# A ninth table looked up by products, gapless sample groups, and the move of the interactions cut into 36 two-dimensional parts

## What is computed

```python
e = jnp.stack([tbl_0[ids[:, 0]], ..., tbl_25[ids[:, 25]]], axis=1)   # 2048 x 26 x 128
combined = concatenate([e, r_dense_x[:, None, :]], axis=1)            # 2048 x 27 x 128
z = einsum('bfd,bgd->bfg', combined, combined)[:, TRIU_I, TRIU_J]     # 351 pairs, k=1
h = concatenate([z, r_dense_x], axis=1)                               # 479 columns
h = maximum(h @ W_top1 + b_top1, 0)                                   # 512
h = maximum(h @ W_top2 + b_top2, 0)                                   # 256
y = h @ W_top3
```

## Time and profile before

| | |
|---|---|
| median of 3 runs | 408.6 us (408.58 to 408.74) |
| the profiled execution | 406.5 us, span 404.7 us, mean granted clock 0.996 |
| TensorE busy | 370.7 us (92%) |
| GpSimd busy | 278.8 us (69%), 288 gathers |
| VectorE busy | 248.3 us (61%) |
| ScalarE busy | 233.8 us (58%) |
| chain that ended last | 49% GpSimd's gathers, 25% TensorE, 16% issue |

### The profile page before, as it was taken

The page is one execution under the profiler, slowest core; times in us unless marked ns, Lnnn a source line. Parts: engine busy times, 40 slices in busy tenths (PEclk is TensorE's granted clock), DMA queues, the critical chain, the costliest instruction groups (busy, mean ns, idle before and its releaser), DMA issues.

```text
span 404.7 us, 8016 instructions
## 1 busy us (share of the span) xinstructions
PE 370.7 (92%) x2976; PEld 349.6 (86%) x2976; DVE 248.3 (61%) x714; ACT 233.8 (58%) x429; POOL 278.8 (69%) x294
## 2 busy tenths in 40 slices
PE   4998978878897899999999999999999999889987
PEld 2787978777886899989999999989999899878976
DVE  5886998458583567647693658647683667223321
ACT  3267846545464656676565756575565655467534
POOL 5777777777777777777777777777777777773000
PEclk9999999989999999999999999999999999999999
DMA  7981132223222223222222222232322222122000
GB/s 209 260 253 45 48 100 55 56 67 96 55 53 71 67 57 83 54 74 64 79 62 70 69 66 72 57 84 57 78 62 72 67 67 74 52 72 52 15 19 2
DMA packets 21637, 30.54 MB, mean 75 GB/s; under 512 B 6960, under 2 KB 15864, under 8 KB 21472
## 3 DMA queue, kind: packets, MB, share of 16 engines
q0 software_dynamic: 9216, 18.89, 17.9%
q1 hardware_dynamic: 12041, 10.91, 10.3%
q10 hardware_dynamic: 343, 0.24, 0.2%
HBM read 26.86 MB, written 0.01 MB: 66 GB/s over the span
## 4 chain that ended last, share of the span: by engine, by line
POOL 49%; PE 25%; issue 16%; ACT 3%; DMA 3%; DVE 2%; POOLq 0%; ACTq 0%
POOL rows L265 49%; PE ps_mlp L347 5%; PE ps_gram L338 4%; PE ps_feat L314 4%; PE ps_feat L317 3%; PE ps_feat L319 3%; DMA rows<-in_tbl,ids_now 2%; PE ps_feat L281 1%; DVE hot L768 1%; ACT feat L528 1%; PE ps_feat L354 1%; PE ps_mlp L414 1%; ACT feat L541 1%; PE ps_gram L354 1%; PE ps_mlp L354 1%
## 5 line engine op out<-in xcount | busy, mean ns | idle before, releaser
L265 POOL DMA_INDIRECT rows<-in_tbl,ids_now x288 | 278.2, 966 | 89.8 <-issue 85.3
L768 DVE TENSOR_SCALAR hot<-ids_all,row_no 125x256 fp32r<-125x256 f32 x512 | 160.6, 384 | 19.4 <-PE ps_feat L319 11.3
L338 PE MATMUL ps_gram<-feat 128*123 128x108 f32 x1024 | 121.8, 274 | 6.8 <-ACT feat L528 4.6
L338 PEld LDWEIGHTS ps_gram<-feat 128*123 128x123 f32 x1024 | 116.8, 190 | 10.2 <-ACT feat L528 5.6
L317 PE MATMUL ps_feat<-hot,table_hi 125*128 125x256 f32 x480 | 118.0, 287 | 3.2 <-ACT feat L528 2.2
L319 PE MATMUL ps_feat<-hot,table_lo 125*128 125x256 f32 x480 | 115.2, 281 | 0.0
L514 DVE COPY z<-ps_gram 27x208 f32<-27x208 f32 x128 | 46.9, 367 | 92.7 <-PE ps_gram L338 91.6
L317 PEld LDWEIGHTS ps_feat<-hot,table_hi 125*128 125x128 f32 x480 | 90.4, 188 | 6.7 <-ACT feat L528 4.7
L319 PEld LDWEIGHTS ps_feat<-hot,table_lo 125*128 125x128 f32 x480 | 90.4, 188 | 0.0
L528 ACT COPY feat<-ps_feat 128x512 f32<-128x512 f32 (+1 forms) x80 | 78.0, 978 | 6.2 <-PE ps_feat L281 5.5
L514 ACT COPY z<-ps_gram 27x208 f32<-27x208 f32 x128 | 41.6, 325 | 50.1 <-PE ps_gram L338 49.3
(11 more groups left out here) (59 smaller groups left out, 307.9 us busy)
## 6 DMA issues: line engine op xcount, KB each, us to landing
rows<-in_tbl,ids_now POOLq DMA_INDIRECT x288, 2.5
table_lo_before<-in_tbl SPq DMA_DIRECT2D x8, 448.0 KB
dense<-in_dense_t SPq DMA_DIRECT2D x8, 128.0 KB
w_lo_before<-in_w SPq DMA_DIRECT2D x1, 1024.0 KB
zp_lo_before<-in_dense_t SPq DMA_DIRECT2D x8, 128.0 KB
zp_lo_before<-z SPq DMA_DIRECT2D x15, 39.0 KB
zp_lo_before<-z SPq DMA_DIRECT2D x15, 36.0 KB
w_lo_before<-in_w SPq DMA_DIRECT2D x1, 512.0 KB
```

Of the source, the lines that this page charges most:

```text
L265: nc.gpsimd.indirect_dma_start(rows[:, row_at(t, f), :], None, gathered[f], bass.IndirectOffsetOnAxis(ap=ids_now[:, t, f:f + 1], axis=0),) ...
L338: mm = nc.tensor.matmul(ps_gram[at % 2][0:FOUR, c, 0:4 * F], four[:, 0:FOUR], four.rearrange("d (j f) -> d j f", f=FPAD)[:, :, 0:F], start ...
L768: op = nc.vector.tensor_scalar(hot[0:VROWS, u % HOTS, c, :], ids[0:VROWS, k, :], row_no[0:VROWS, no + UNIT * i + c:no + UNIT * i + c + 1], ...
```

## The change

- **Nine kept tables.** A table with 1250 rows joins, as a single of 10 chunks (`CHUNKS = [8] * 8 + [10]`), so `PAIRS` is 5, the fifth with one table, and 17 tables are gathered (272 loads), the last group being one table. `look_up(h, 4)`, `build(h, 4)`, `empty_pair(h, 4)` and a fifth spreading, of 256 columns, are added. `HOTS` is 9.
- **No gaps.** A sample has 27 columns of `feat`, four have 108; the products are 107 by 104 columns, and the zeros at the start are no longer written.
- **Copies.** A batch is taken by one engine, VectorE the even ones, ScalarE the odd ones, with four copies. In the last batch each takes four of the eight products. [...]
- **z and zp.** `z` holds two tiles, `zp` holds 32 samples of three chunks in a row. The nine rectangles become 36 moves of two dimensions a tile. For the last tile SP issues 17, ScalarE 11 and GpSimd 8.
- **ids.** `ids_few` lies on `ids_few_no`, so its load waits for the memset, and later for the spreadings; it comes in three moves. The load for half 1 stands behind the weights. `y` lies in `hid2`.
- **The start's order** on all engines; the last two pieces of the diff are TensorE's and VectorE's.

```diff
-CHUNKS = [8] * 8
+CHUNKS = [8] * 8 + [10]
-HOTS = 10
+HOTS = 9
...
-FPAD = 32
-FOUR = 3 * FPAD + F
+FOUR = 4 * F
+LOWER = F - 1
+GROUPED = P // 4
+FROM_ROW = (0, 0, 0, 64)
+PLACE = (0, 1, 2, 0)
+PLACES = 3
...
+PACKS = [(i, j) for i in range(len(RECTS)) for j in range(4)]
+LAST_BY_SP, LAST_BY_ACT, LAST_BY_POOL = PACKS[:17], PACKS[17:28], PACKS[28:]
...
+        def pack_rects(eng, t, rects, done=None):
+            h = t // 2
+            eng.wait_ge(z_by_dve, BATCHES // 2 * (t + 1) + (t == TILES - 1))
+            eng.wait_ge(z_by_act, BATCHES // 2 * (t + 1))
+            for i, j in rects:
+                (g, height), at, to = RECTS[i], RECT_AT[i], THREE * (4 * (t % 2) + j)
+                eng.dma_start(zp[h % 2][at:at + height, to:to + THREE],
+                              z[F * j:F * j + height, PLACES * (t % 2) + PLACE[j], GROUPED * (g - 1):GROUPED * (g - 1) + THREE]
+                              ).then_inc(done or packed[t % 2], 16)
...
                 if h > 0:
-                    sp.wait_ge(ids_few_ready, h)
-                sp.dma_start(ids_few[:], ids_kept[:, h * HALF:(h + 1) * HALF].rearrange("(p k) s -> p k s", k=2)
+                    sp.wait_ge(ids_spread, PAIRS * h)
+                else:
+                    sp.wait_ge(constants_set, 2)
+                at = slice(h * HALF, (h + 1) * HALF)
+                sp.dma_start(ids_few[0:PAIRS - 1, :, :], ids_kept[0:KEPT - 1, at].rearrange("(p k) s -> p k s", k=2)
                              ).then_inc(ids_few_landed, 16)
+                for k in range(2):
+                    sp.dma_start(ids_few[PAIRS - 1:PAIRS, k, :], ids_kept[KEPT - 1:KEPT, at]).then_inc(ids_few_landed, 16)
...
                 if at >= 2:
-                    pe.wait_ge(z_by_act, at - 1)
-                    pe.wait_ge(z_by_dve, at - 1)
+                    pe.wait_ge([z_by_dve, z_by_act][at % 2], at // 2)
                 for c in range(BATCH):
-                    four = x[:, P * (BATCH * b + c):P * (BATCH * b + c + 1)]
-                    mm = nc.tensor.matmul(ps_gram[at % 2][0:FOUR, c, 0:4 * F], four[:, 0:FOUR],
-                                          four.rearrange("d (j f) -> d j f", f=FPAD)[:, :, 0:F], start=True, stop=True)
+                    four = x[:, FOUR * (BATCH * b + c):FOUR * (BATCH * b + c + 1)]
+                    mm = nc.tensor.matmul(ps_gram[at % 2][0:FOUR - 1, c, 0:4 * LOWER], four[:, 0:FOUR - 1],
+                                          four.rearrange("d (j f) -> d j f", f=F)[:, :, 1:F], start=True, stop=True)
...
+        def copy_products(eng, copy, done, t, b, groups=range(BATCH)):
+            at = BATCHES * t + b
+            eng.wait_ge(gram_done, at + 1)
+            if t >= 2 and b < 2:
+                eng.wait_ge(packed[t % 2], PACK * (t // 2))
+            first, stop = groups[0], groups[-1] + 1
+            for j in range(4):
+                rows_of = slice(FROM_ROW[j], F * j + LOWER)
+                to = z[rows_of, PLACES * (t % 2) + PLACE[j], :].rearrange("p (g c) -> p g c", c=GROUPED)
+                op = copy(to[:, :, BATCH * b + first:BATCH * b + stop],
+                          ps_gram[at % 2][rows_of, first:stop, LOWER * j:LOWER * (j + 1)].rearrange("p c g -> p g c"))
...
-            for p in range(PAIRS):
+            for p in range(3):
                 spread_ids(0, p)
             for n in range(PAIRS):
                 look_up(0, n)
                 turn(0, n)
-            turn(0, PAIRS)
-            spread_ids(1, 0)
-            spread_ids(1, 1)
+                if n + 3 < PAIRS:
+                    spread_ids(0, n + 3)
+            for p in range(3):
+                spread_ids(1, p)
...
             build(0, 0)
             build(0, 1)
+            split_table(4)
+            split_table(5)
             build(0, 2)
-            for n in range(WHOLE_FIRST, KEPT):
-                split_table(n)
+            split_table(6)
+            split_table(7)
+            split_table(8)
+            build(0, 3)
             put_dense(0)
-            build(0, 3)
+            build(0, 4)
             split_table(0)
             split_table(1)
+            build(1, 0)
             take(0, 0)
             split_table(2)
-            take(0, 1)
-            build(1, 0)
             split_table(3)
             take(0, 2)
-            take(0, 3)
```

More of the change, by code:

```diff
@@ L55 @@
 RECT_AT = [sum(x[1] for x in RECTS[:n]) for n in range(len(RECTS))]
-LAST_BY_SP = 6
 ZP_CHUNKS = 4
-PACK = 16 * len(RECTS)
+THREE = WIDTH * GROUPED
+DENSE_AT = WIDTH * HALF
+PACK = 16 * 4 * len(RECTS)
+PACKS = [(i, j) for i in range(len(RECTS)) for j in range(4)]
+LAST_BY_SP, LAST_BY_ACT, LAST_BY_POOL = PACKS[:17], PACKS[17:28], PACKS[28:]
 OUTS = 7
 def feat_turns():
-    order = [("ids", 0, n) for n in range(PAIRS)]
+    order = [("ids", 0, n) for n in range(3)]
     for n in range(PAIRS):
-        order += [("pair", 0, n), ("tile", 0, n)]
-    order += [("tile", 0, PAIRS), ("ids", 1, 0), ("ids", 1, 1)]
+        order += [("pair", 0, n), ("tile", 0, n)] + [("ids", 0, n + 3)] * (n + 3 < PAIRS)
+    order += [("ids", 1, n) for n in range(3)]
     for t in range(1, TILES):
@@ L167, in bass_dlrm_tower @@
         z_by_act, z_by_dve = sem("z_by_act"), sem("z_by_dve")
-        packed = [sem(f"packed{i}") for i in range(4)]
+        packed = [sem(f"packed{i}") for i in range(2)]
+        packed_by_pool = sem("packed_by_pool")
         packed_dense = [sem(f"packed_dense{i}") for i in range(2)]
@@ L666, in last_odd @@
                 h = t // 2
-                take(t - 1, 0)
                 empty_turn(t, 0)
@@ L709, in _ @@
             number_ids(1)
-            for n in (2, 3):
-                split_table(n)
+            split_table(0)
+            split_table(1)
             empty_pair(0, 3)
             empty_turn(0, 3)
+            split_table(2)
+            split_table(3)
+            empty_pair(0, 4)
             empty_turn(0, 4)
-            empty_ids(1, 0)
-            empty_ids(1, 1)
+            for p in range(3):
+                empty_ids(1, p)
             odd(1)
@@ L778, in put_dense, with take, rest_zp @@
                      dense[:, P * (t % 2):P * (t % 2 + 1)].rearrange("d (j c) -> d j c", j=4)).then_inc(dense_put, 1)
-            def take(t, b):
-                copy_products(dve, copy, (0, 1), z_by_dve, t, b)
-            def rest_zp(h, part=0, chunks=slice(0, ZP_CHUNKS), samples=slice(0, HALF)):
+            def take(t, b, groups=range(BATCH)):
+                copy_products(dve, copy, z_by_dve, t, b, groups)
+            def rest_zp(h, part=0, columns=slice(0, ZP_CHUNKS * HALF)):
                 if h < 0:
@@ L786, in rest_zp @@
                 dve.wait_ge(zp_hi_ready, h + part + 1)
-                rest(zp_lo[h % 2][:, chunks, samples], zp[h % 2][:, chunks, samples], zp_hi[:, chunks, samples]
+                rest(zp_lo[h % 2][:, columns], zp[h % 2][:, columns], zp_hi[:, columns]
                      ).then_inc(zp_lo_ready, 1)
@@ L799, in even @@
                 rest_hid1(h - 3, 3)
-                take(t - 1, 1)
                 build(h, 3)
@@ L809, in odd @@
                 h = t // 2
-                for b in range(BATCHES):
-                    take(t - 1, b)
+                take(t - 1, 0)
+                take(t - 1, 2)
                 put_dense(t)
@@ L841, in _ @@
             nc.vector.memset(ids_few_no[:].bitcast(F32), 0.0).then_inc(constants_set, 1)
-            for i in range(FEATS):
-                nc.vector.memset(feat[i][:].rearrange("d (s f) -> d s f", f=FPAD)[:, :, F:FPAD], 0.0
-                                 ).then_inc(pads_ready, 1)
             dve.wait_ge(row_no_ready, len(SIZES))
```

148 lines of the change are left out of this document (70 added, 78 removed).

## The result

The changed kernel takes **516.25 us** (median of 5 runs, 512.65 to 517.19) against 408.58 for the kernel before on the same chip: ratio 1.264, 95% interval 1.259 to 1.268. The forecast was 414.6, range 408 to 428: the sign was right, the size wrong by 102 us. The profiled execution took 512.65 us, with a span of 510.8.

What follows compares the result with a forecast made beforehand. GpSimd's gathers were taken to bind, with TensorE the bound close behind. Start +8.7, later steps -6.5 and end +3.8 gave +6.0 on the profiled 406.5, so 412.5; the median, 2.1 higher, became 414.6 us, range 408 to 428.

Steps and rivals of the forecast that it cites:

- The moves: z to zp on SP: 36 moves at 0.44 us each, 15.9 us a tile, hidden in the middle.
- The threshold: Moves on SP: the cover that hides them is gone at 0.63 us a move.
- The rival: SP's issue of 36 moves binds: some 490 us in all; chance 0.05, shared with z reused too early.
- The pitch: TensorE's product records: pitch falls from 107 to near 94 ns, 0.86 us a tile, -12.9 over 15 tiles.
- Gathers: TensorE's 10.9 us of waiting for gathered rows goes entirely; GpSimd then waits over 10 us for TensorE.
- The steady steps: TensorE in the middle: even steps of 21.9 us and odd ones of 23.2 us.
- The start: Up to step 2: late ids and VectorE's order make step 2 begin at 66.8 instead of 58.08, +8.7 us.
- the upper bound: Start: the clock may fall to its lower level after TensorE idles before batch 2, making the start +10.4 us.
- The end: After the last products: issuing the last tile's moves delays the last layer 1, +3.8 us (from +2 to +6).
- The sign: Whole kernel: +6.0 us, about 1.5 per cent slower; chance of slower 0.84.
- the steps: TensorE's work and waits from the second step to the end: sum -6.5 us.
- The upper bound of 18 ns for the pitch: Product records: largest saving if both operands shorten the pitch in proportion, 14 to 18 ns a record.

Runs made afterwards that it cites:

- Experiment 3: Changed kernel with 36 moves, but block 1 read from off-chip memory, block 2 moving 512 B rows and block 3 256 B rows; run once, 494.13 us.
- experiment 1: Changed kernel with 9 moves a tile instead of 36, each four times as wide, three quarters of packed values another sample's; 404.88 us, ratio 0.991.
- experiment 2: Changed kernel with 27 moves a tile, one double-width move replacing two, some values another sample's; 425.53 us, ratio 1.045.
- 5: Kernel before with nine tables and the changed kernel's start and engine orders, keeping padded products and 9 moves; 415.73 us, ratio 1.016.
- experiment 7: Kernel of experiment 1 with VectorE copying batch 0 before building the first pair of half 1; 403.13 us, ratio 0.987.
- 8: Kernel of experiment 1 with VectorE taking the low parts of w1 and w2 at the end of step 3; 398.67 us, ratio 0.975.
- experiment 10: Changed kernel with its 36 on-chip moves a tile replaced by 4 writes to off-chip scratch and 9 three-dimensional loads; all computed; 410.49 us, ratio 1.003.
- 11: Kernel of experiment 10 with VectorE copying batch 0 before half 1's first pair and taking w1's and w2's low parts after step 3; 402.97 us, 0.983.

## Why the prediction was wrong, step by step

- **The moves: the step that failed.** "The new moves are nearest to these: 36 x 0.44 = 15.9 us a tile." Measured 0.75 each, 27 a tile. I put the old moves' 0.83 down to their third dimension and took the price of two-dimensional loads; but those loads came from off-chip memory, and the row of the very same pair, z to zp, was the 0.83. At least two things differed between the rows, and I let the smaller one explain the whole price. Experiment 3 gives about 0.22 us for an on-chip instead of an off-chip source, experiment 1 some 0.07 for the third dimension of the old moves (0.79 in the median, 0.72 now). That leaves 0.1 of the 0.4 between the old moves and the table loads (0.40 in the median), which no run takes apart. The row of w2 could have warned me.
- **The threshold agrees with all runs, and none tests it closely.** "Gone at 0.63 us a move" is 23 us a tile. In the middle 20.5 us a tile are hidden (experiment 2); 25.7 (experiment 3) and 27 (after) are not.
- **The rival happened.** "Issue of 36 moves binds ... some 490", with a chance that should have been far over 0.05, since the nearest row of this pair stood over the threshold. Its sum was short too, by some 20 us: it left out the 60 us before the first move and the other issues. By the rows: 60.2 to the first, six halves of 56.4, and 112.0 from 398.82 to the end, 510.8.
- **What the wait became.** TensorE is idle 510.8 - 390.7 = 120.1 us, in experiment 1's kernel 401.6 - 373.1 = 28.5: 91.6 us. The other 17.6 of the 109.2 between the spans are TensorE's own work made longer, at a mean clock of 0.903 instead of 0.992. The rival had no such part.
- **The pitch: right.** 94 ns in the trace; the steps lost 0.88 and 0.8 to 1.0 us for my 0.86 a tile (experiments 1 and 5). It only pays beside the ninth table, which the prediction has (relief of GpSimd "is worth those 10.9 us and no more").
- **Gathers: right.** No wait for them in after or in experiment 1, where GpSimd waits 14.4 us for TensorE.
- **The steady steps: nearly.** Forecast 21.9 and 23.2; experiment 1 has 21.3 to 21.45 and 22.8 to 22.95. From step 2 to step 16 that kernel is 8.7 us shorter than before, and I had -6.5 with everything in it.
- **The start: mechanism right, size 2.4 too high in this trace.** Step 2 at 64.34, +6.3 (forecast +8.7, bounds 4.0 to 10.4). First products 42.84 for 44.9, batch 2 at 48.46 for 51.5. The wait for VectorE's first copy is there (2.01 us), and experiment 7 removes it. The size depends on the clock, as the upper bound had it: six traces have this start, and in the three in which the clock fell to 0.50 after that wait (experiments 3, 8 and 10) step 2 begins at 65.6 to 66.6, in the others (after, experiments 1 and 2) at 63.7 to 64.5.
- **The end.** Forecast +3.8 at 0.44 a move. In after the last layer 1 waits 11.3 us for zp, at 0.75 a move; at the 0.44 that I assumed the end can't be measured. From its last product to the last layer 1 are 28.0 us, not the 12 of the forecast. With 9 moves the last step is 25.90 us against 26.72 before, with the scratch 28.16 in experiment 10 and 30.75 in 11, where TensorE was granted 0.50 from 387.0 to 393.8.
- **The sign.** With moves that cost little the change is faster by 0.9 per cent (experiment 1), not slower by 1.5: the start by 2.4 us, the steps by 2.2 and the end by up to 4.6 were all taken too high. That kernel has 9 moves, not 36 cheap ones, so its end says least about my sum. "Slower" came true by luck, for a reason that I gave one chance in twenty.
- **Slips in the sum.** 0.43 / 4 is 0.108, not 0.109, and 23 / 36 is 0.64, not 0.63; neither changes the forecast. The upper bound of 18 ns for the pitch is not worked out anywhere: 107 x 16 / 123 gives 14.

Open: what sets the price of an issue. On-chip to off-chip 0.37 (26 rows of 3328 B), off-chip to on-chip 0.50 for 384 B rows and 0.78 in three dimensions with four such pieces a row, on-chip to on-chip 0.72 at 384 and at 1536 B a row. No single one of source, dimensions or bytes orders these four.

## What to carry to other kernels

Before one transfer is split into several, price an issue by the row with the same two memories, and multiply: at 36 a tile, 0.3 us of error is 11 us a tile. Two rows that differ in two things can't tell which sets the price; look for a third row that differs in one. Measure the two halves of a change together as well as apart: here shorter products were worth nothing while GpSimd bound, and relief of GpSimd cost 7 us more than it brought until the products were shortened.

## What the runs showed of the hardware

- An on-chip to on-chip move of 14 to 26 rows cost SP's queue 0.70 to 0.78 us, one of 2 rows 0.57 to 0.64, with rows of 256, 384 or 1536 B alike; a write of 26 rows from on-chip to off-chip 0.37. A detour through off-chip memory with 13 issues was cheaper than 36 direct ones.
- GpSimd issued such moves faster than SP. Its eight have 26 and 2 rows, for which SP's medians in after are 0.74 and 0.59 us:

```profile
L216 POOL DMA_DIRECT2D zp_lo_before<-z x8 | 4.1, 518 | 48.2 <-DVE z L546 48.2
```

- In waits of about 10 us in after the granted clock fell to 0.50 and stayed there for the first work behind them (197.8 to 208.0 above); 16 product records took 3.20 us at that level instead of 1.66. The 4.75 us wait in experiment 1 was followed by it too, the 2.01 us wait in the start in three traces of five. A stall could thus be worth more than its length: without the one of 4.75 us step 3 is 6.2 shorter.
- A copy of 208 columns took VectorE 362 ns with 26 rows, 377 with 43 and 351 with 80 in after: the rows that are copied along and that nobody reads cost next to nothing.
